# Two dense feed-forward stages: where a block's activation is split into high and low part

## The reference, cut to what matters

```python
# inside _L3_attn_ref, after its attention
x2 = _layer_norm(x, ln2_g, ln2_b)
h = jax.nn.relu(x2 @ w1 + b1)            # 128 -> 512
x = x + (h @ w2 + b2)                    # 512 -> 128
# _L3_ffn_ref, the last step of the network
h = jax.nn.relu(jnp.einsum('bsh,hi->bsi', hidden_states, W1) + b1)
return jnp.einsum('bsi,ih->bsh', h, W2) + b2
```

## Time and profile before

| | |
|---|---|
| median of 3 runs | 961.03 us (960.5 to 966.48) |
| profiled execution, its own time | 960.05 us |
| its span | 958.2 us |
| mean granted TensorE clock | 0.896 |
| busy: PE, PEld | 753.1 us (79%), 476.1 us (50%) |
| busy: DVE, ACT, POOL | 723.6 us (76%), 552.2 us (58%), 419.6 us (44%) |

### The profile page before, as it was taken

The page is one execution under the profiler, slowest core; times in us unless marked ns, Lnnn a source line. Parts: engine busy times, 40 slices in busy tenths (PEclk is TensorE's granted clock), DMA queues, the critical chain, the costliest instruction groups (busy, mean ns, idle before and its releaser), DMA issues. The chain is left out here.

```text
span 958.2 us, 11018 instructions
## 1 busy us (share of the span) xinstructions
PE 753.1 (79%) x3292; PEld 476.1 (50%) x3292; DVE 723.6 (76%) x1730; ACT 552.2 (58%) x865; POOL 419.6 (44%) x449
## 2 busy tenths in 40 slices
PE   1769998789889799889468988867788776677776
PEld 1546775345536577666356766642232222223554
DVE  7958886798997657785767567769998787874675
ACT  1035665657564456544126766767899887774333
POOL 7215664624533034454716666634333124303554
PEclk9969999979896789999769999988999888888799
DMA  5100000100000000000100000000000000000001
GB/s 157 33 1 23 15 14 14 34 22 23 20 21 12 1 1 0 1 1 0 34 0 1 1 1 1 1 0 1 0 1 1 1 1 1 1 1 0 1 0 45
DMA packets 9611, 11.60 MB, mean 12 GB/s; under 512 B 720, under 2 KB 5712, under 8 KB 9552
## 3 DMA queue, kind: packets, MB, share of 16 engines
q1 hardware_dynamic: 9552, 10.89, 3.9%
HBM read 9.84 MB, written 1.05 MB: 11 GB/s over the span
## 5 line engine op out<-in xcount | busy, mean ns | idle before, releaser
L869 POOL TENSOR_TENSOR rbuf<-B,rbuf 128x512 fp32r<-128x512 f32 x154 | 200.8, 1307 | 185.4 <-ACT rbuf L794 121.0
L839 DVE TENSOR_TENSOR B<-B,spread_bank 128x512 f32<-128x512 f32 x128 | 87.0, 682 | 43.7 <-ACT B L786 31.0
L794 ACT ACTIVATE rbuf<-B 128x512 fp32r<-128x512 f32 x132 | 83.0, 628 | 44.6 <-PE y_bank L620 33.1
L618 PE MATMUL y_bank<-rbuf,WH 128*128 128x512 f32 x174 | 74.9, 430 | 26.2 <-POOL rbuf L869 15.6
L786 ACT ACTIVATE B<-gate_banks,WR 128x512 f32<-128x512 f32 x96 | 66.0, 688 | 36.2 <-PE gate_banks L620 27.2
L826 DVE TENSOR_TENSOR B<-B,up_banks 128x512 f32<-128x512 f32 x68 | 46.4, 682 | 47.9 <-PE up_banks L620 29.7
L474 POOL TENSOR_SCALAR small<-small 128x4 f32<-128x4 f32 x36 | 7.5, 209 | 169.7 <-DVE small L373 169.2
L618 PE MATMUL gate_banks<-XH,WH 128*128 128x512 f32 x168 | 76.1, 453 | 2.5 <-ACT YT L1190 0.8
L783 ACT ACTIVATE B<-gate_banks 128x512 f32<-128x512 f32 x68 | 40.7, 599 | 51.8 <-PE gate_banks L620 50.7
L619 PE MATMUL y_bank<-rbuf,WH 128*128 128x512 f32 x174 | 69.7, 401 | 0.0
L620 PE MATMUL y_bank<-rbuf,WL 128*128 128x512 f32 x174 | 69.7, 401 | 0.0
(11 more groups left out here) (273 smaller groups left out, 2040.8 us busy)
## 6 DMA issues: line engine op xcount, KB each, us to landing
STG<-in_w_split SPq DMA_DIRECT2D x27, 256.0 KB, 2.7
X<-in_x SPq DMA_DIRECT2D x4, 256.0 KB, 4.8
out<-X SPq DMA_DIRECT2D x4, 256.0 KB, 2.3
WR<-in_w_raw SPq DMA_DIRECT2D x1, 524.5 KB, 4.2
STG<-in_w_exact SPq DMA_DIRECT2D x2, 256.0 KB, 2.7
STG<-in_w_split SPq DMA_DIRECT2D x5, 64.0 KB, 1.8
STG<-in_w_split SPq DMA_DIRECT2D x1, 192.0 KB, 2.3
STG<-in_w_split SPq DMA_DIRECT2D x1, 128.0 KB, 2.1
```

The lines of the kernel that those rows point to most:

```text
L618: nc.tensor.matmul(dst, w[0], x[0], start=start, stop=False)
L794: nc.scalar.activation(rbuf[n % 2][:, :], HO[n % 3], ACT.Copy).then_inc(hh_ready, 1)
L839: nc.vector.tensor_tensor(HO[n % 3], src, SP[:, :], ALU.mult).then_inc(h_ready, 1)
L869: e_.tensor_tensor(rbuf[2 + n % 2][:, :], AO[n % 2] if f.dense else HO[n % 3], rbuf[n % 2][:, :].bitcast(F32), ALU.subtract).then_inc(hl_r ...
```

## The change

In the two dense stages ScalarE runs the ReLU of each bank twice: first into `rbuf[n % 2]`, which rounds it to the high part, and then into `AO[n % 2]`. VectorE's cast is gone; VectorE makes the low part of every block, and GpSimd none. The wait for `down_done` goes with the high part to ScalarE, ahead of it; the wait for `hl_ready` stays ahead of the write of `AO`. `act_done`, which frees the bank for `up`, is raised by the second of the two. The gated and the routed stages keep their code.

```diff
--- before.py
+++ after.py
@@ -776,13 +776,19 @@
             def act(c, b):
                 n = block_no(f, c, b)
                 a.wait_ge(first_full, n + 1)
-                if in_stage(f, c, b, 2):
-
-                    a.wait_ge(hl_ready if f.dense else mul_done if f.gate else h_ready, n - 1)
                 if f.gate:
+                    if in_stage(f, c, b, 2):
+                        a.wait_ge(mul_done, n - 1)
                     nc.scalar.activation(AO[n % 2], G[n % 2][:, :], ACT.Silu).then_inc(act_done, 1)
                 else:
                     bias = {"ffn2": "b1_2", "ffn3": "b1_3", "ffn4": "fb1"}[f.key]
+                    if f.dense:
+                        if in_stage(f, c, b, 2):
+                            a.wait_ge(down_done, n - 1)
+                        nc.scalar.activation(rbuf[n % 2][:, :], G[n % 2][:, :], ACT.Relu, bias=raw(bias, b, 1))\
+                            .then_inc(hh_ready, 1)
+                    if in_stage(f, c, b, 2):
+                        a.wait_ge(hl_ready if f.dense else h_ready, n - 1)
                     nc.scalar.activation(AO[n % 2], G[n % 2][:, :], ACT.Relu, bias=raw(bias, b, 1))\
                         .then_inc(act_done, 1)
 
@@ -841,11 +847,7 @@
             def split(c, b):
                 n = block_no(f, c, b)
                 v.wait_ge(act_done, n + 1)
-                if in_stage(f, c, b, 2):
-                    v.wait_ge(down_done, n - 1)
-                nc.vector.tensor_copy(rbuf[n % 2][:, :], AO[n % 2]).then_inc(hh_ready, 1)
-                if not low_on_pool(f, c, b):
-                    low(nc.vector, v, f, n)
+                low(nc.vector, v, f, n)
 
             for b in range(f.blocks):
                 if f.gate:
@@ -871,7 +873,7 @@
 
         def low_on_pool(f, c, b):
 
-            return c * f.blocks + b < NC * f.blocks - 2
+            return not f.dense and c * f.blocks + b < NC * f.blocks - 2
 
         def ffn_pool(g, chain, f, c, hook, work):
             for b in range(f.blocks):
```

## The result

The changed kernel takes 970.14 us (median of 8 runs, 963.1 to 971.5) against 960.67 before: ratio 1.0083, with a 95% interval of 1.0053 to 1.0113. Slower, by 0.5 to 1.1%. The ratios compare the means of the runs; the medians lie 9.5 us apart, or 1.0%. Forecast were 968.7 and a range of 961 to 976. Measured again beside the experiments it was 970.33 (ratio 1.0102, 1.0063 to 1.0141).

What follows compares the result with a forecast made beforehand. No engine is full in the last two stages; latency loops through ScalarE and VectorE close each slot. Slot changes sum to +7.2 on 960.05, 967.3, plus 1.4 for clock: 968.7 us, range 961 to 976.

Steps and rivals of the forecast that it cites:

- one more stretch at the lower clock: 1.4 us added to 967.3 for one more low-clock stretch, as TensorE idles 2.5 us ahead of the transposes.
- T0 to down(0): From the transposes' start (T0): ScalarE's high(1), activation(1), result put down(0) at T0+4.04 for 2.86, +1.2 per slot.
- down(0) to the next T0: Second half of a slot, 6.67: VectorE's saving of 1.5 nearly spent on the extra activation and waiting for down(1).
- The slots at full clock: Slots of the last two stages at full clock: 10.7 in the last stage, 11.4 in the one before.
- The first row, 9.9: Slot 872.76 to 883.50: nothing waits for a result, VectorE's relief counts in full, 10.74 becomes 9.9, -0.8.
- The clock term: TensorE's lower clock costs 1.4 per slot hit, kept in the second, third and fifth row after the first.
- The second activation is not hidden: Denies the rival that ScalarE takes the 32 activations in its idle time: -2.9, 957.2 us; chance 0.12.
- The clock alone: Rival that TensorE's clock falls further, all slots losing 1.4 and second halves paying too: 981 us; chance 0.13.
- both sides cancel: Rival that waits on down(1) and down(3) are met more often, 0.5 to 1 per slot: 962 us; chance 0.15.
- Busy time: ScalarE's up by some 22; VectorE's up 19 for low parts, down some 17 and 6, about 4 lower in all.
- holds nobody else for long: GpSimd's low part (L869) waits 63 us for VectorE's cast and is said to hold up little else.
- charge nothing: No cost for low parts beside GpSimd's small operations; the skill's rule would add 0.9, giving 969.6.

Runs made afterwards that it cites:

- the wait moved: Changed kernel with ScalarE writing the activation first and the high part, with its wait for the down, behind it: 960.98 us, ratio 1.0008.
- the wait gone: Changed kernel with four pairs of high and low buffers in place of two, same instructions and order: 957.23 us, ratio 0.9966.
- both kernels filled: Six unread 512-column matmuls added in TensorE's wait: changed kernel 965.75 us, ratio 1.0057; kernel before 959.57 us, ratio 0.9985.
- the high part alone: Changed kernel with the low part put back on GpSimd, so only the high part has moved to ScalarE: 962.31 us, ratio 1.0014.

## Why the prediction was right

The mechanism is as forecast: the write took its wait for a down to ScalarE, where the result stood behind it. The runs with the wait moved, and with the wait gone, show it. That the time was met within 1.4 us is in part luck, as the slots show (clock in brackets; the seventh row runs from the sixth start of the transposes to the end, the last is the sum, and the 1.4 that was added for one more stretch at the lower clock belongs to no row):

| before | forecast | execution of 963.1 | execution near the median |
|---|---|---|---|
| 10.74 (0.86) | 9.9 | 8.74 (1.00) | 9.96 (0.83) |
| 10.77 (0.93) | 11.4 | 11.42 (1.00) | 11.41 (0.96) |
| 11.92 (0.78) | 12.8 | 11.38 (1.00) | 14.71 (0.68) |
| 10.98 (0.84) | 13.0 | 12.58 (0.86) | 13.73 (0.75) |
| 10.22 (0.98) | 10.4 | 11.51 (0.85) | 10.46 (1.00) |
| 11.13 (0.87) | 12.1 | 11.89 (0.86) | 10.69 (1.00) |
| 19.68 (0.99) | 22.9 | 22.74 (0.93) | 23.77 (0.87) |
| 85.44 | 92.5 | 90.26 | 94.73 |

- **T0 to down(0), +1.2 per slot.** 4.04 forecast, 4.04 measured in the slot shown and 4.00 to 4.05 in the others at or near full clock, with the three activations in the order it named. The second digit is luck: down(3) ended 0.03 later than in its walk, and the activations stood 0.58 apart and not 0.60. With both activations of block 1 off the way of the result the time was 957.96, and with only the wait gone 957.23.
- **down(0) to the next T0.** 6.67 forecast, 6.65 measured. VectorE's relief came as worked out (four normalising instructions 1.11, low part 0.69) and went for the extra activation and the wait on down(1). The new line waits for `y_bank` L620, as the text had asked for.
- **The slots at full clock.** 11.4 and 10.7 came out as 11.38 to 11.42 and 10.69, and the first chunk of the last stage, 10.4, as 10.46. The first row, 9.9, was reached only at a clock of 0.83; at full clock it took 8.74.
- **The clock term** was the weakest. It put the third, fourth and sixth at the lower clock and left the first as it was. The third kept the full clock in one execution (11.38 for 12.8) and the sixth in the other (10.69 for 12.1), and the fifth lost it in one (11.51 for 10.4), while the slots of 14.71 and 13.73 are 3.3 and 2.1 above their length at full clock (11.4 as measured, 11.6 as forecast), not 1.4. In the third slot the clock was low at down(0), 5.64 behind T0 for 4.0, and the half behind it took 9.07 for 7.4: the second half paid too. That the median was met (968.7 against 970.14) rests on these misses cancelling. Nor did TensorE's wait ahead of T0, by which the last 1.4 was argued, decide it: after waits of 3.18 and 3.19 one slot (891.20) kept the full clock and another (894.54) had 0.68.
- **The rivals.** The second activation is not hidden: it is queued behind exactly the wait that the argument against it named. The clock alone is not the answer, since 6.2 stay with both kernels filled. Nor did both sides cancel: 20.4 of the 26.0 that L788 waits are for a down.
- **Busy time.** On the page of the profile VectorE's busy time went from 723.6 to 718.1 (about 4 less were forecast) and ScalarE's from 552.2 to 570.0. That is 18 more and not 22: L788 and L792 add up to 43.8 for the 22.1 of one line before, but a queued activation starts some 0.1 before its predecessor ends, and the page counts that once. None of it was a guide to the time.
- **One loose reading.** That GpSimd's low part "holds nobody else for long" does not fit the kernel before: of the 28.6 that its L786 waited in these stages, 8.3 were for L869, and TensorE's downs waited 4.3 for it. That can be part of why the low part alone on VectorE was a gain.

## What to carry to other kernels

When a write moves to another engine, its wait for a free buffer moves too, and in an in-order queue everything behind it inherits that wait; price the work behind it (here the activation and the result), not the engine's idle share. Put what others wait for first, or give the write a deeper ring of buffers: either turned 0.8 to 1.0% slower into 0.3 to 0.4% faster with the same instructions. Test the parts of a change alone and together: here one alone was a gain, the other made no difference, and both together were a loss. And before moving a step earlier, ask what it waits for itself.

## What the runs showed of the hardware

Whether GpSimd and VectorE slow each other goes by size and by order here. A residual add with two inputs in SBUF took 1.16 for 0.69 beside GpSimd's low part of 128x512 (fence of the high part alone). A low part on VectorE at 939.83 took its 0.69 with the power of 128x4 (939.13, 1.01) beside it, and so did the add of the earlier trace rows. The Trainium skill, "SBUF — State Buffer", section "Who interferes with whom", says that a VectorE instruction with two inputs in SBUF contends with a GpSimd instruction that reads SBUF. The trace agrees for the large operation, by 0.47 us; for the small one VectorE was not held up, so the prediction's choice to charge nothing stands.

The order of the two matters as well, and here it is GpSimd that waits. In the three kernels that have only the low part moved to VectorE (with and without the moves in the layer norm), the power took 1.46 to 1.56 in the 14 places where it started 0.10 or 0.11 behind a low part of VectorE, and 1.01 in the other 4. In the changed kernel every low part near a power starts behind it, and the power took 1.01 in all 12 places of the two executions.

A row of four normalising instructions is not slowed evenly. In the kernel before one of them lasts 0.34 in the median and 1.32 at the most; where GpSimd is silent none is above 0.35.

Filling TensorE's wait with unread matmuls went with a higher clock: over the runs the mean granted clock of the span was 0.898 against 0.892 for the changed kernel, and 0.900 against 0.895 for the kernel before. By the medians the changed kernel got 4 to 5 us shorter and the kernel before 1.7; by the ratios the former is 2.5 to 4.3, with intervals that touch. It didn't prevent every fall: the filled kernels still have slots of 0.75 and 0.85. What makes it fall in one slot and not in the next was not settled.
